# Routing each batch inside the transformer part, with fixed regions of the row buffer for each expert

## The chip, the cores and the metric

The kernel runs on one NeuronCore of a Trainium2 chip. Its time is the device time of one execution in microseconds (us), lower is better. Engines are TensorE (PE; PEld is its weight load), VectorE (DVE), ScalarE (ACT), GpSimd (POOL) and SyncE (SP, which here issues nearly all DMAs).

## The reference

Eight batches of 512 tokens of width 256 go through two layers. The first has two attentions with quantised operands (self, then cross over a context) and a gated feed-forward. The second has a causal self-attention, a cross-attention, and a mixture of eight experts, of which each token uses its two best:

```python
router_weights = jax.nn.softmax(xf @ rw + rb, axis=-1)
topw, topi = jax.lax.top_k(router_weights, K)          # K = 2
topw = jax.nn.softmax(topw, axis=-1)
combine = jnp.zeros((T, E)).at[jnp.arange(T)[:, None], topi].add(topw)
h = gelu(jnp.einsum('td,edf->etf', xf, w1) + b1[:, None, :])
eo = jnp.einsum('etf,efd->etd', h, w2) + b2[:, None, :]
out = jnp.einsum('etd,te->td', eo, combine)
x = layernorm(x + out)
```

T is 4096 tokens, E 8 experts, D 256 and FF 1024.

## The kernel before

There are two parts, one after the other, each a block in which every engine has its own instruction list; the second starts when all engines have ended the first.

**`transformer`** does everything up to the last layer norm ahead of the experts, in batches. `program_steps` names every job as (kind, batch B, stage s, number n) with the jobs it must follow; `program_order` puts the jobs of all engines into one order, `ORDER`, by list scheduling: at each turn it takes, among the jobs that could start earliest, the one with the longest way to the end (`to_end`), with durations from `TAKES` and `LANDS`. Where TensorE would stand idle for `WARM_GAP`, it inserts a filler multiplication (kind `W`, L1286), which keeps the clock up. Each engine then walks `ORDER` and issues its own jobs, in order, with semaphore waits (`after`). Two streams are interleaved: a quantised attention of one batch (S scores, M and nb the row maximum, E the exponential, Q the quantisation on GpSimd at L1000, T and ev the transposed probabilities) and an exact attention of another (A, am, B, E2, AV2). The stages of a batch are 0, 1 (quantised), 2 (feed-forward), 3, 4 (exact), 5 (the norm ahead of the experts; its kinds are rs, xn, gb on GpSimd). Kind `ST` stores the batch to `mid` in DRAM (L914). The batch itself lives in `X`, three buffers. Weights come through the ring `wring` in pieces of 256 KB, `RING` = 8 pieces in flight: piece i is loaded when piece i - 8 has been used for the last time. SP's list also holds `psk`/`pkk`, the store and reload of split queries and keys; beside each of the first 20 stores it writes 528 KB of empty rows into `rows_in` (`fill_some_rows`, L872).

**`experts`** first routes all 4096 tokens at once. `mid` is loaded back into `moe_x` (L1561); TensorE turns it (L1689) and multiplies it with the router weights (L1701); VectorE finds the two best experts of each token (L1822 to L1851), two multiplications with a triangle and with ones give counts, and from them come `owner`, the expert of each of `BLOCKS` = 39 blocks of 256 rows (`OWNERS_READY`), and `slot_of`, the row of each token's two copies (`SLOTS_READY`). Experts' rows are packed: an expert's first row follows from the counts of all batches. GpSimd then scatters the rows, 128 to an indirect DMA, 64 DMAs (L1640). SP, which has meanwhile issued the weights of four blocks, waits for all of them:

```python
sp.wait_ge(s_r, OWNERS_READY)
for slot in range(WSLOTS):
    load_weights(slot, slot)
sp.wait_ge(s_sc, 16 * 2 * NTILES)
for slot in range(2):
    load_block(slot, slot)
```

Then the loop over 39 blocks: TensorE turns a block's rows (L1717), multiplies with `w1` (L1733), ScalarE applies GELU (L1783), TensorE multiplies with `w2` (L1743), VectorE adds the bias (L1894), GpSimd scatters the result to `rows_out` by token (L1650). A tail gathers both results of each token, adds them with their weights and normalises. Empty rows carry a destination out of bounds, so they are not written.

## Time and profile before

| | |
|---|---|
| median of 3 runs | 3555.44 us (3551.76 to 3558.73) |
| the profiled execution | 3552.56 us |
| its span, first to last instruction | 3550.8 us |
| mean granted TensorE clock | 0.926 |
| busy over the span | PE 85%, PEld 48%, DVE 59%, ACT 54%, POOL 46% |
| end of the last tile of batch 7 | 2699.2 us |
| first instruction of the expert part | 2702.56 us |
| first expert multiplication | 2858.62 us |

Shares over the whole span mix the two parts, so stretches are to be read one by one. A granted clock of 1.00 is 2.4 GHz and 0.50 is 1.2 GHz.

### The profile page before, as it was taken

The numbers are of one execution on the slowest core, as the hardware profiler recorded it, in microseconds if no ns is written. First come the engines' busy times: TensorE is split into PE (matmuls) and PEld (weight loads), VectorE is DVE, ScalarE is ACT, GpSimd is POOL, SyncE is SP. The second block draws the span as 40 slices with busy tenths as digits, with TensorE's granted clock in tenths as the row PEclk, the third lists the DMA queues.
The fourth block names the chain that finished last, engine by engine and source line by source line (L and its number), as shares of the span: only waits on it lengthen the run. The fifth ranks groups of instructions, "written<-read, shape, count | busy, mean of one in ns | idle before, by whom it ended". The sixth has DMA issues, their size and how long they took to land. (4 is left out here: it accounts for less than half of the span.)

```text
span 3550.8 us, 54838 instructions
## 1 busy us (share of the span) xinstructions
PE 3008.0 (85%) x18111; PEld 1698.6 (48%) x18111; DVE 2094.1 (59%) x4305; ACT 1905.0 (54%) x3883; POOL 1631.3 (46%) x2840
## 2 busy tenths in 40 slices
PE   6888999898899998899998889988886079999990
PEld 3435444543544454354445435543435067777770
DVE  4877887786789678778967877765450100000006
ACT  4665767576666767666675767654441022232221
POOL 4655554673666368366636736462221511111114
PEclk9999999999999999999999999889986589999995
DMA  3004221531342142132304222242312434555524
GB/s 87 16 25 108 62 68 31 117 82 39 83 83 54 30 96 53 41 68 62 70 24 101 49 48 61 51 77 52 58 29 69 177 128 161 171 176 164 163 94 142
DMA packets 268695, 290.23 MB, mean 82 GB/s; under 512 B 32366, under 2 KB 254190, under 8 KB 268320
## 3 DMA queue, kind: packets, MB, share of 16 engines
q1 hardware_dynamic: 259904, 270.05, 30.5%
q0 software_dynamic: 6816, 17.06, 1.3%
q8 instruction: 134, 2.20, 0.3%
q14 instruction: 113, 0.93, 0.1%
q10 hardware_dynamic: 1728, 0.01, 0.0%
HBM read 225.70 MB, written 62.97 MB: 81 GB/s over the span
## 5 line engine op out<-in xcount | busy, mean ns | idle before, releaser
L1253 ACT ACTIVATE probs<-ps,nbias,sc 128x512 f32<-128x512 f32 x1024 | 790.8, 778 | 276.0 <-DVE nbias L1134 216.9
L1000 POOL TENSOR_SCALAR pq<-probs,rstep 128x512 f16<-128x512 f32 x1024 | 709.6, 693 | 245.4 <-PE ps L1367 161.2
L1151 DVE TENSOR_REDUCE m<-ps 128x1 f32<-128x512 f32 (+3 forms) x1024 | 561.2, 583 | 292.1 <-PE ps L1393 150.3
L1131 DVE TENSOR_REDUCE nmax<-ps 128x2 f32<-128x1024 f32 x512 | 620.9, 1213 | 93.5 <-PE ps L1359 92.8
L1390 PE MATMUL ps<-kst,qst 96*128 96x512 bf16 (+3 forms) x1024 | 328.9, 352 | 92.3 <-issue 50.6
L1893 DVE COPY to<-moe_in 128x1 uint32 x78 | 12.0, 154 | 648.1 <-PE moe_ps L1743 648.1
L1143 DVE TENSOR_SCALAR big<-ps 128x1024 bf16<-128x1024 f16 x512 | 348.2, 680 | 60.7 <-PE ps L1367 59.5
L1367 PE MATMUL ps<-id,pq 128*128 128x128 f16 x4096 | 329.7, 226 | 47.1 <-DVE big L1143 40.0
L1412 PE MATMUL ps<-qst,kst 108*128 108x512 bf16 (+3 forms) x1024 | 305.8, 352 | 66.5 <-ACT big L1272 31.2
L1367 PEld LDWEIGHTS ps<-id,pq 128*128 128x128 f16 x4096 | 261.3, 101 | 193.5 <-issue 129.1
L1272 ACT ACTIVATE big<-ps 128x512 f32<-128x512 f32 (+3 forms) x640 | 275.0, 482 | 145.1 <-PE ps L1415 93.4
L1783 ACT ACTIVATE hT<-moe_ps,e_b 128x256 f32<-128x256 f32 x312 | 147.0, 473 | 360.1 <-PE moe_ps L1733 360.0
L1650 POOL DMA_INDIRECT rows_out<-yb,to x78 | 76.7, 984 | 532.5 <-DVE yb L1894 528.4
L1733 PE MATMUL moe_ps<-moe_bT,e_w 128*128 128x256 f32 x1248 | 287.5, 388 | 8.6 <-ACT hT L1783 7.7
L1743 PE MATMUL moe_ps<-e_w,hT 128*128 128x256 f32 x1248 | 279.4, 382 | 15.4 <-ACT hT L1783 13.1
L1337 PE MATMUL ps<-xT,wring 128*128 128x512 f32 x512 | 272.3, 640 | 0.5 <-ACT xT L1191 0.2
L1743 PEld LDWEIGHTS moe_ps<-e_w,hT 128*128 128x128 f32 x1248 | 233.9, 190 | 54.7 <-issue 23.4
L1733 PEld LDWEIGHTS moe_ps<-moe_bT,e_w 128*128 128x128 f32 x1248 | 219.9, 190 | 70.0 <-ACT hT L1783 32.8
L1390 PEld LDWEIGHTS ps<-kst,qst 96*128 96x128 bf16 x1024 | 98.0, 99 | 316.3 <-DVE m L1151 176.8
L1359 PE MATMUL ps<-kmask,qi 32*128 32x512 bf16 x1024 | 205.4, 401 | 45.5 <-ACT probs L1253 30.6
L1429 PE MATMUL ps<-big,v_f 128*32 128x512 f32 (+3 forms) x2048 | 231.0, 528 | 2.7 <-ACT big L1272 1.6
L1286 PE MATMUL ps<-idb 128*128 128x512 bf16 x737 | 206.6, 392 | 22.0 <-DVE sc L1048 18.1
(202 smaller groups left out, 4610.0 us busy)
## 6 DMA issues: line engine op xcount, KB each, us to landing
e_w<-in_L_xattn_e_w_dram SPq DMA_DIRECT2D x78, 1024.0 KB, 7.8
wring<-in_L_xattn_ff_w_dram SPq DMA_DIRECT2D x96, 256.0 KB, 2.8
parts<-parts_sb SPq DMA_DIRECT2D x64, 384.0 KB, 3.2
kst<-parts SPq DMA_DIRECT2D x192, 128.0 KB, 4.8
qst<-parts SPq DMA_DIRECT2D x192, 128.0 KB, 5.1
moe_in<-rows_in SPq DMA_DIRECT2D x39, 264.0 KB, 2.7
rows_in<-zero SPq DMA_DIRECT2D x19, 528.0 KB, 4.3
xn<-in_ctx_dram SPq DMA_DIRECT2D x16, 512.0 KB, 3.9
```

The source lines that it names most:

```text
L1000: nc.gpsimd.tensor_scalar(pq[:, u % 2, h, :], probs[:, u % 2, h, :], rstep[:, u % 2, h:h + 1], HALF_ROUND, ALU.mult, ALU.add).then_inc(SIG ...
L1131: nc.vector.tensor_reduce(nmax[:, n % 2, :], ps[:, a:a + 2, :], AX.X, ALU.max, negate=True).then_inc(SIG["M"], 1)
L1143: nc.vector.tensor_scalar(probs_t[:, g % 2, 2 * p:2 * p + 2, :, t * P:(t + 1) * P], PT, -HALF_ROUND, WMAX, ALU.add, ALU.min).then_inc(SIG[ ...
L1151: nc.vector.tensor_reduce(m32[:, g % 2, t, h:h + 1], bank(("A", B, s, n))[:, 0:width], AX.X, ALU.max, negate=True).then_inc(SIG["am"], 1)
L1253: nc.scalar.activation(probs[:, u % 2, h, :], ps[:, BANKS[("S", B, s, u)][h], :], ACT.Exp, bias=nbias[:, u % 2, h:h + 1], scale=sc[:, s:s ...
L1272: last = nc.scalar.activation(ex[:, half, h, j, i0:N], ps[:, from_, i0:N], ACT.Exp, scale=SCALE)
L1337: last = nc.tensor.matmul(bank(e), wt[:, k, (f % 2) * P:(f % 2 + 1) * P], xT[:, k, :], start=(k == 0), stop=(k == KT - 1))
L1367: last = nc.tensor.transpose(PT[:, h, j, :], pq[:, n % 2, h, j * P:(j + 1) * P], id16[:, :])
L1390: last = nc.tensor.matmul(bank(e)[:, 0:width], qst[0:PAIR_ROWS, head, t * P:(t + 1) * P], kst[0:PAIR_ROWS, head, 0:width], start=True, sto ...
L1412: last = nc.tensor.matmul(dst[:, i0:N], kst[0:rows_, head, jt * P:(jt + 1) * P], qst[0:rows_, head, i0:N], start=True, stop=not causal(s))
L1733: last = nc.tensor.matmul(ps[:, f % 2, 0:BLOCK], w1[:, ws, k, f * P:(f + 1) * P], bT[:, slot, k, :], start=(k == 0), stop=(k == KT - 1))
L1743: last = nc.tensor.matmul(ps[:, 2 + 2 * slot + s, 0:D], hT[:, f, s * P:(s + 1) * P], w2[:, ws, f, :], start=(f == 0), stop=(f == FT - 1))
```

## The change

The routing leaves the expert part and becomes ten new kinds of job of stage 6 of each batch in the planned order: `rT`, `dr` (turn the batch's rows and drain them), `rL` (logits), `rl`, `rx`, `rm`, `ry`, `ri` (softmax, two best, weights, destinations), `rP` (prefix counts within the batch, by small multiplications), `rp` (the row of each copy, and the running counts `run`), and eight `sc` (indirect DMAs from GpSimd). An expert no longer has packed rows: expert e owns the fixed region of 4096 rows from 4096 e, and `run` says how far it is filled. `rows_in` has 135 blocks in place of 39, and all of it, with a last part of seven blocks, is filled with empty rows beforehand: 64 fills of 528 KB, eight a batch, and one of 1.9 MB after the last batch's store. `sc` of batch B waits for that batch's eight fills. The transformer part now ends when the last scatter has landed. `X` has four buffers, each row eight elements wider for the destinations; the weight ring has six pieces. The expert part computes `owner` from `run`, and `place`, the block in `rows_in` of each of the 39 blocks; it loads weights 0, row blocks 0 and 1, weights 1 to 3, and only then `mid`, which only the tail needs.

```diff
+REGION = TOKENS // BLOCK
+ALL_BLOCKS = NE * REGION + NE - 1
+X_DEEP = 4
...
-RING = 8
+RING = 6
...
-ON = {"PE": "W S T AV A MT B AV2 xT cT k q v y g w z",
-      "DVE": "M nb R ev am n1 n3 st dy dz ki qi vi dV dw",
-      "ACT": "E do mt E2 dT dc dk dq dv dg ge",
-      "POOL": "Q ms n2 rs xn gb bi spk spq",
+ON = {"PE": "rT rL rP W S T AV A MT B AV2 xT cT k q v y g w z",
+      "DVE": "rl rm ri rp M nb R ev am n1 n3 st dy dz ki qi vi dV dw",
+      "ACT": "dr rx ry E do mt E2 dT dc dk dq dv dg ge",
+      "POOL": "sc Q ms n2 rs xn gb bi spk spq",
...
+TAKES = {"rT": 0.49, "dr": 0.66, "rL": 1.4, "rl": 0.55, "rx": 0.25, "rm": 1.2, "ry": 0.25, "ri": 2.2, "rP": 0.6, "rp": 1.0, "sc": 1.25,
...
-        step("LX", B, 0, 0, ("ST", B - 3, 5, 0) if B >= 3 else None)
+        step("LX", B, 0, 0, *((("ST", B - X_DEEP, 5, 0), ("sc", B - X_DEEP, 6, 2 * NT - 1)) if B >= X_DEEP else ()))
...
+        for m in range(KT):
+            step("rT", B, 6, m, ("gb", B, 5, NT - 1), B and ("rL", B - 1, 6, 0))
+            step("dr", B, 6, m, ("rT", B, 6, m))
+        step("rL", B, 6, 0, ("dr", B, 6, KT - 1))
+        step("rl", B, 6, 0, ("rL", B, 6, 0), B and ("rp", B - 1, 6, 0))
+        step("rx", B, 6, 0, ("rl", B, 6, 0))
+        step("rm", B, 6, 0, ("rx", B, 6, 0))
+        step("ry", B, 6, 0, ("rm", B, 6, 0))
+        step("ri", B, 6, 0, ("ry", B, 6, 0))
+        step("rP", B, 6, 0, ("ri", B, 6, 0))
+        step("rp", B, 6, 0, ("rP", B, 6, 0))
+        for n in range(2 * NT):
+            step("sc", B, 6, n, ("rp", B, 6, 0), *(("ps" + which, B, z, m) for which in "kq" for z in (3, 4) for m in range(KT)))
...
+                if B >= X_DEEP:
+                    sp.wait_ge(s_stored, 16 * (B - X_DEEP + 1))
+                    sp.wait_ge(s_sc[B % X_DEEP], 16 * 2 * NT * (B // X_DEEP))
+                sp.dma_start(X[:, B % X_DEEP, :, 0:D], x[B].rearrange("(t p) d -> p t d", p=P)).then_inc(s_x[B % X_DEEP], 16)
...
+            def fill_rows(e, c):
+                first, many = (e * TOKENS + c * N, NT) if c < NBATCH else (NE * TOKENS, (NE - 1) * BLOCK // P)
+                sp.dma_start(every_row[first:first + many * P, :].rearrange("(p n) d -> p n d", p=P),
+                             zero[:, :].unsqueeze(1).broadcast_to([P, many, ROW])).then_inc(s_zeroed[c], 16)
...
-                    fill_some_rows()
+                    fill_rows(filled[0] % NE, filled[0] // NE)
+                    filled[0] += 1
...
+            fill_rows(0, NBATCH)
+            sp.wait_ge(s_zeroed[NBATCH], 16)
+            for i in range(X_DEEP):
+                sp.wait_ge(s_sc[i], 16 * 2 * NT * ((NBATCH - i + X_DEEP - 1) // X_DEEP))
...
+                if kind == "sc":
+                    k, t = n // NT, n % NT
+                    after(pool, "rp", B, s)
+                    pool.wait_ge(s_zeroed[B], 16 * NE)
+                    nc.gpsimd.indirect_dma_start(rows_in.rearrange("b r d -> (b r) d"),
+                                                 bass.IndirectOffsetOnAxis(ap=slot_of[:, B, k, t:t + 1], axis=0),
+                                                 X[:, B % X_DEEP, t, :], None).then_inc(s_sc[B % X_DEEP], 16)
...
+                if kind == "rl":
+                    after(dve, "rL", B, s)
+                    rest_loaded(dve)
+                    then(nc.vector.tensor_tensor(lg[:, :, :], bank(("rL", B, s, 0))[:, 0:NT * NE].rearrange("p (t e) -> p t e", e=NE),
...
+                if kind == "rp":
+                    after(dve, "rP", B, s)
+                    filled = bank(("rP", B, s, 0))
+                    then(nc.vector.tensor_tensor(pos[:, :, :], filled[:, 0:NT * NE].rearrange("p (t e) -> p t e", e=NE),
+                                                 every_tile(run[:, :]), ALU.add), 1)
+                    then(nc.vector.tensor_tensor(run[:, :], filled[:, NT * NE:(NT + 1) * NE], run[:, :], ALU.add), 2)
+                    for k in range(2):
+                        last = nc.vector.tensor_tensor(at_pos[:, k, :, :], eq[:, k, :, :], pos[:, :, :], ALU.mult)
+                    then(last, 3)
+                    then(nc.vector.tensor_reduce(slot_f[:, :, :], at_pos[:, :, :, :], AX.X, ALU.add), 4)
+                    then(nc.vector.tensor_copy(slot_of[:, B, :, :], slot_f[:, :, :]), 5)
...
+                if kind == "dr":
+                    src = ("rT", B, s, n)
+                    after(act, *src)
+                    if n == 0 and B:
+                        after(act, "rL", B - 1, s)
+                    nc.scalar.activation(rT[:, n, :], bank(src), ACT.Identity).then_inc(SIG["dr"], 1)
+                if kind == "rx":
+                    after(act, "rl", B, s)
+                    nc.scalar.activation(pr[:, :, :], lg[:, :, :], ACT.Exp).then_inc(SIG["rx"], 1)
+                if kind == "ry":
+                    after(act, "rm", B, s)
+                    nc.scalar.activation(e1[:, :], dlt[:, :], ACT.Exp).then_inc(SIG["ry"], 1)
...
+                if kind == "rT":
+                    after(pe, "gb", B, 5, NT - 1)
+                    bank_free(pe, e)
+                    for t in range(NT):
+                        last = nc.tensor.transpose(bank(e)[:, t * P:(t + 1) * P], X[:, B % X_DEEP, t, n * P:(n + 1) * P], id32[:, :])
+                    last.then_inc(SIG["rT"], 1)
+                if kind == "rL":
+                    after(pe, "dr", B, s, KT - 1)
+                    rest_loaded(pe)
+                    bank_free(pe, e)
+                    for t in range(NT):
+                        for k in range(KT):
+                            last = nc.tensor.matmul(bank(e)[:, t * NE:(t + 1) * NE], rT[:, k, t * P:(t + 1) * P], rw[:, k, :],
+                                                    start=(k == 0), stop=(k == KT - 1))
+                    last.then_inc(SIG["rL"], 1)
+                if kind == "rP":
+                    after(pe, "ri", B, s)
+                    bank_free(pe, e)
+                    flat = chosen[:, :, :].rearrange("p t e -> p (t e)")
+                    nc.tensor.matmul(bank(e)[:, 0:NT * NE], earlier[:, :], flat, start=True, stop=False)
+                    for t in range(1, NT):
+                        nc.tensor.matmul(bank(e)[:, t * NE:NT * NE], ones[:, :], flat[:, 0:(NT - t) * NE], start=False, stop=(t == NT - 1))
+                    for t in range(NT):
+                        last = nc.tensor.matmul(bank(e)[:, NT * NE:(NT + 1) * NE], ones[:, :], flat[:, t * NE:(t + 1) * NE],
+                                                start=(t == 0), stop=(t == NT - 1))
+                    last.then_inc(SIG["rP"], 1)
...
-            for c in range(NB):
-                sp.dma_start(xs[:, c * NT:(c + 1) * NT, 0:D], mid[c].rearrange("(t p) d -> p t d", p=P)).then_inc(s_x[c], 16)
...
             def load_block(j, slot):
-                sp.dma_start(xin[:, slot, :, :].unsqueeze(1), rows_in[bass.ds(j, 1)].rearrange("a (s p) d -> p a s d", p=P)).then_inc(s_in[slot], 16)
+                b = sp.value_load(place[0:1, bass.ds(j, 1)], min_val=0, max_val=ALL_BLOCKS - 1)
+                sp.dma_start(xin[:, slot, :, :].unsqueeze(1), rows_in[bass.ds(b, 1)].rearrange("a (s p) d -> p a s d", p=P)).then_inc(s_in[slot], 16)
 
             sp.wait_ge(s_r, OWNERS_READY)
-            for slot in range(WSLOTS):
-                load_weights(slot, slot)
-            sp.wait_ge(s_sc, 16 * 2 * NTILES)
+            load_weights(0, 0)
+            sp.wait_ge(s_r, PLACES_READY)
             for slot in range(2):
                 load_block(slot, slot)
+            for slot in range(1, WSLOTS):
+                load_weights(slot, slot)
+            for c in range(NB):
+                sp.dma_start(xs[:, c * NT:(c + 1) * NT, :], mid[c].rearrange("(t p) d -> p t d", p=P)).then_inc(s_x[c], 16)
...
-            pool.wait_ge(s_r, SLOTS_READY)
-            for c in range(NB):
-                pool.wait_ge(s_x[c], 16)
-                for t in range(c * NT, (c + 1) * NT):
-                    for k in range(2):
-                        nc.gpsimd.indirect_dma_start(rows_in.rearrange("b r d -> (b r) d"),
-                                                     bass.IndirectOffsetOnAxis(ap=slot_of[:, k, t:t + 1], axis=0),
-                                                     xs[:, t, :], None).then_inc(s_sc, 16)
...
+            then(nc.vector.tensor_tensor(started_first[:, :, :], started[:, :, :],
+                                         first[:, :].unsqueeze(1).broadcast_to([P, BLOCKS, NE]), ALU.mult))
+            then(nc.vector.tensor_reduce(owner_first[:, :], started_first[:, :, :], AX.X, ALU.max))
+            then(nc.vector.scalar_tensor_tensor(out=place_f[:, :], in0=owner_f[:, :], scalar=float(REGION), in1=iota_b[:, :],
+                                                op0=ALU.mult, op1=ALU.add))
+            then(nc.vector.tensor_tensor(place_f[:, :], place_f[:, :], owner_first[:, :], ALU.subtract))
+            then(nc.vector.tensor_copy(place[:, :], place_f[:, :]))
+            assert steps[0] == PLACES_READY
```

## Rows read from the trace of the kernel before

**Rows 1.** Stretches: us, then busy us of PE, PEld, DVE, ACT, POOL, PE clock, DMA share, GB/s.
```profile
1400.00:1800.00 400.00, 366.39 (x2296) 178.15 (x2292) 313.80 (x601) 266.86 (x516) 220.29 (x400) 0.97 0.28 59
...
2750.00:2800.00 50.00, 1.30 (x6) 0.72 (x5) 18.78 (x136) 0.65 (x2) 21.86 (x23) 0.50 0.62 227
2800.00:2850.00 50.00, 0.00 (x0) 0.00 (x0) 0.00 (x0) 0.00 (x0) 37.86 (x40) 0.50 0.29 106
...
3200.00:3300.00 100.00, 95.41 (x440) 77.91 (x439) 6.71 (x26) 30.84 (x62) 12.79 (x13) 1.00 0.53 172
```

**Rows 2.** The timeline where one part ends and the next begins: start, duration, engine, line.
```profile
2698.49 0.72 POOL L982 TENSOR_TENSOR X<-X,row_l_ln_b 128x256 f32<-128x256 f32 x1
...
2702.56 0.21 POOL L1620 MEMSET moe_id<- 128x128 f32 x1 [3.35 <-POOLq L634]
...
2704.46 0.43 SPq L1559 DMA_DIRECT2D e_b<-in_L_xattn_e_b_dram  x1
...
2712.00 0.10 DVE L1804 MEMSET credit<- 128x1 f32 x2 [22.89 <-DMA e_b<-in_L_xattn_e_b_dram]
```

**Rows 3.** The chain that ended last, from 2700 to 2900: start, duration, what.
```profile
2713.46 3.65 PE moe_ps L1689 x16
2717.11 1.70 PE moe_ps L1701 x16
...
2771.14 85.55 issue
2856.69 1.10 PE moe_ps L1717 x4
...
2858.62 2.08 PE moe_ps L1733 x4
...
2876.78 7.12 PE moe_ps L1733 x32
```

**Rows 4.** The line of the scatter: duration in ns, minimum, median, maximum, then first and last start.
```profile
L1640 POOL DMA_INDIRECT rows_in<-moe_x,slot_of x64: 956/960/1242, 2771.4 to 2851.3; - x64
...
DMA to landing us min/median/max: 2.4/2.4/6.5
```

**Rows 5.** SP's timeline, the stores of batches 0 to 3 to mid.
```profile
689.47 0.37 SPq L914 DMA_DIRECT2D mid<-X  x1
...
1006.38 0.37 SPq L914 DMA_DIRECT2D mid<-X  x1
...
1316.64 0.37 SPq L914 DMA_DIRECT2D mid<-X  x1
...
1630.91 0.37 SPq L914 DMA_DIRECT2D mid<-X  x1
```

**Rows 6.** DMA issues of the page: the zero fills, KB each, median us to landing.
```profile
rows_in<-zero SPq DMA_DIRECT2D x19, 528.0 KB, 4.3
```

**Rows 7.** Timeline of VectorE in the routing: one step on 8, one on 312 elements.
```profile
2765.59 0.17 DVE L1860 TENSOR_SCALAR nblk<-incl 128x8 f32<-128x8 f32 x1
...
2766.41 0.48 DVE L1865 TENSOR_TENSOR started<-iota_b,first 128x312 f32<-128x312 f32 x1
```

**Rows 8.** Owners, first weight load, bandwidth from 2700 to 2900 (5 us each), issues of e_b1.
```profile
2767.66 0.18 DVE L1869 CAST owner<-owner_f 128x39 int32<-128x39 f32 x1
...
2768.86 0.40 SPq L1568 DMA_DIRECT2D e_w<-in_L_xattn_e_w_dram  x1
...
GB/s 107 253 365 357 133 4 0 0 0 3 0 2 0 7 324 385 400 398 409 342 103 106 106 105 102 108 108 108 108 108 86 104 0 0 0 86 332 113 83 329
...
L1563 SPq DMA_DIRECT2D e_b<-in_L_xattn_e_b_dram x8: 582/678/2798, 2716.2 to 2726.0; - x8
```

**Rows 9.** Groups by line, 600 to 2600: count, busy us, mean ns, idle before.
```profile
L1286 PE MATMUL ps<-idb 128*128 128x512 bf16 x376 | 99.6, 386 | 0.9 <-ACT xT L1191 0.9
```

**Rows 10.** Lines of the quantisation (from 600 to 2600) and of nbias: ns minimum, median, maximum.
```profile
L1000 POOL TENSOR_SCALAR pq<-probs,rstep x740: 687/692/715, 600.8 to 2357.0; 128x512 f16<-128x512 f32 x185
...
L1134 DVE TENSOR_SCALAR nbias<-nmax,sc x512: 196/229/1146, 51.7 to 2351.8; 128x2 f32<-128x2 f32 x171
```

299 lines of the change are left out of this document (122 added, 177 removed), and 1 row of the table TAKES.

## The prediction

> **What bounds the kernel now.** I read the stretches first, because an average over the span mixes a transformer part with an expert part. In the transformer part, to 2699 us, TensorE is busy 0.92 of the time (366 of 400 us), VectorE 0.78, GpSimd 0.55; in the expert part TensorE is at 0.95 and sets the pace alone [rows 1]. Between them lie two stretches with TensorE at 0.03 and at nothing, where in the second only GpSimd does anything [rows 1]. That hole is where the change acts. The timeline gives its two ends: the last normalised tile of batch 7 is finished at 2699.21 (2698.49 + 0.72) and stored, and the expert part's first instruction is at 2702.56 [rows 2]. The chain of waits tells what fills the rest: eight batches read back, turned and multiplied with the router weights from 2713.46 on, the choice on VectorE, which ends at 2771.1, and then 85.55 us that the chain can only call issue, until TensorE turns the first block at 2856.69 [rows 3]. The source line of the scatter explains those 85.55 us: 64 indirect DMAs on GpSimd from 2771.4 to 2851.3, one every 1.27 us (79.9 / 63), each landing 2.4 us after its start, and SP loads no block before all have landed [rows 4]. So the path from 2699.2 to the first expert matmul at 2858.62 [rows 3] is serial, and 159.4 us long, of which the expert part's share is 156.1 (from 2702.56).
>
> **What is not on the path.** In the transformer part the period from one batch's store to the next is 316.9 us (689.47 to 1006.38), then 310.3 (to 1316.64) and 314.3 (to 1630.91) [rows 5]. Each batch has eight places for a zero fill and there are 20 fills, so the first of these periods holds eight and the other two none: a fill costs at most (316.9 - 312.3) / 8 = 0.6 us, though 4.3 us pass until it has landed [rows 6]. The change has 44 more of them: at most 25 us, at least nothing; since 310.3 and 314.3 differ by as much without any fill, I take nothing.
>
> **Sum, part 1: the head of the expert part shrinks.** Removed: 8 loads of mid ahead of everything, the 8 turned chunks, the logits, the choice, the 64 scatters. What is left ahead of the first expert matmul, counted from the part's first instruction T0:
> - SP issues the e_b2 load (1 MB) as its third DMA. Before it was the fifth, at 2704.46, and VectorE got past it at 2712.00, 7.5 us later [rows 2]. Two small DMAs earlier (0.95 us), that is T0 + 8.5.
> - VectorE's steps to OWNERS_READY: seven on 8 to 39 elements at 0.17 and two on 312 elements at 0.48 [rows 7], with about 0.04 between: 2.5, so T0 + 11.0. Five more to PLACES_READY, two of them on 312: 1.7, so T0 + 12.7, hidden behind SP.
> - SP reads the owner and issues the first weights 1.0 us after OWNERS_READY, as before (2767.84 to 2768.86) [rows 8]: T0 + 12.0. SP's eight e_b1 issues end before that if they take their median of 0.68 us [rows 8].
> - 2 MB of weights at the 400 GB/s that the queue shows when it is full [rows 8] take 5.2 us, with 2 us of latency 7.2, and the two row blocks (0.5 MB, 1.3 us) are queued behind them: about T0 + 21. I allow 0.5 more for SP's extra register reads.
> - Turning, draining and starting the matmul took 1.9 us (2856.69 to 2858.62): T0 + 23.4.
> So this part gives 156.1 - 23.4 = **132.7 us**. Bounds: the weights 2 us later than 7.2, if the queue is not quite full, and SP late by its e_b1 issues (2716.2 to 2726.0 in this trace, some 10 us for eight behind other loads [rows 8]): 5 us less. Nothing suggests more than 2 us of extra gain.
>
> **Part 2: batch 7's routing now trails the transformer part.** Nothing follows it there that could hide it. From the last tile:
> - 8 transposes, 2 drains, 16 logit matmuls: 0.9 + 0.7 + 1.7 + 0.1 = 3.5 at the fast rate; the rows show 16 transposes in 3.65 at one moment and 16 matmuls in 1.70 at another [rows 3], so a cold TensorE adds up to 2.6.
> - Choice: 24 VectorE instructions on 8 to 32 elements, by the 0.17 of one on 8 [rows 7] about 0.2 with its gap, and one Exp of a like size that is not hidden: 5.0. Eight prefix matmuls at the 0.11 of a logit matmul 0.9; the places, six more small steps, 1.3. Together 10.7.
> - Eight scatters, 7 x 1.27 = 8.9, and 2.4 to land [rows 4].
> That is 22.0 us to T0, with 0.2 for the end of the block, where before it was 3.35: **18.9 us lost**. The last fill (1.9 MB, issued after the store) takes 3.5 x 4.3 = 15 us [rows 6] and ends inside it. Bounds 17 to 24.
>
> **Part 3: routing of batches 0 to 6 inside the transformer part.** Per batch it adds 3.4 us of TensorE, 5.9 of VectorE (25 instructions), 1.7 of ScalarE and 8 x 1.26 = 10.1 of GpSimd, 21 us in all. Its work is nobody's input until the experts, so the planner puts it where an engine would stand idle. Cover: TensorE spends 99.6 us of 2000 on filler multiplications [rows 9], 15.7 a period, besides 0.08 idle; VectorE is idle 0.22 and GpSimd 0.45 of 314 us [rows 1]. Below, the cost is nothing (all in gaps); above, 21 us a batch, if every instruction stood alone on the path. Streams are tightly interlocked: the probabilities quantised on GpSimd (0.69 us each [rows 10]) can have one scatter of 1.27 ahead of each, and eight in a row at worst. I take each instruction to delay its engine's next work by about a fifth of itself, 4 us a batch, nearer to nothing because the eight fills a batch did not show either, and count six batches (batch 6's routing falls after its store, where only batch 7's one stream is left): **24 us lost**. This is the least certain term.
>
> New waits, and what stands behind them: GpSimd's `sc` waits for VectorE's `rp` and for the batch's fills (issued within the batch, long landed), with the quantisation of the next batches behind it, and ScalarE's exponentials behind that; VectorE waits for its own last step 24 times a batch, with row maxima behind; TensorE's `rL` and `rP` wait for ScalarE and VectorE, with every matmul behind. In the plan all are due when reached; the 4 us stand for where they are not. SP's 44 more fill issues stand ahead of the `pkk` reloads, as the first 20 did without a trace in the period. SP's wait of the load of X for scatters is four batches late, so it is free.
>
> **A rule that speaks against part 3.** The 64 scatters that the trace shows ran beside an idle VectorE at 0.96 us [rows 1, 4], and now run beside one busy for 0.78. The nearest row on what the two do to each other: GpSimd's quantisation stays within 687 to 715 ns in 740 cases, while VectorE's tiny nbias takes 196 to 1146 ns [rows 10], so the one that is held up is VectorE, by at most 0.95. If each of 8 scatters did that once, it would be 7.6 us a batch. The Trainium skill (SBUF — State Buffer, on the port pair that VectorE and GpSimd share) says that a DMA issued from GpSimd cannot write its descriptors while VectorE is in a two-port mode, and gives 3100 ns beside one against 620 ns alone. By that page's figures a scatter would take 2.5 us more, 20 us of GpSimd a batch, an estimate; no row here shows it.
>
> **Part 4: small things.** RING 6 in place of 8 loads each weight piece two pieces later; a piece is 256 KB and lands sooner than the 528 KB fill's 4.3 us [rows 6], and a period has 26 pieces, 12 us each, so only the last of a run of pieces is at risk: 0, at worst one wait of 4.3 a batch, 34. Two fewer loads in the start: 0 to 2 us gained, taken as 0. Four X buffers: batch B + 3 is loaded when batch B is stored, a period and more ahead of need, so 0. After the first block, weights 1 to 3 and 4 MB of mid are in the queue ahead of block 2's rows: (6.3 + 4.2) MB / 400 GB/s = 26 us from T0 + 21, so these rows land near T0 + 50, and TensorE wants them 25.3 us after the first matmul (18.2 for block 0, 7.1 into block 1 [rows 3]): T0 + 48.7. **2 us lost**, 0 to 6. From there the expert loop and the tail run as before, with 39 blocks.
>
> **The sum** against the profiled execution's own 3552.6 us (span 3550.8, 2.9 under the median of the runs, 3555.4): 3552.6 - 132.7 + 18.9 + 2 + 24 = 3464.8. I say 3466, for the runs lie a little above the profiled one.
>
> **Rivals.**
> - *All of the routing is hidden* (part 3 nothing): 3552.6 - 132.7 + 18.9 + 2 = 3441. For it: some 40 us of TensorE slack and 140 of GpSimd a period. Against it: a list that is in order and planned with estimates; a mistaken place stalls what is behind it. Chance 0.22.
> - *Routing shows at half its size*, 12 us a batch for six: 3441 + 72 = 3513. Scatters hold VectorE as nbias is held, 7.6, beside the 4 above, or a ring of six makes loads late. Chance 0.15.
> - *Slower than before*: the eight scatters in a row put GpSimd behind, quantisation is late, and with it both streams. The rest of the change gains 3555.4 - 3441 = 114 us, so it takes 114 / 7 = 16.3 us a batch before this decides; GpSimd's added work is 10.1 and all engines' 21, so nearly everything would have to be exposed, or a scatter stretched threefold. At 20 a batch: 3581. Chance 0.05.
> - *The hole is not closed*: something else holds the first block, such as SP's queue. Then perhaps half the 132.7 comes: 3530. Chance 0.03.
> - The forecast, 2 to 8 us a batch: 3464.8, own range 3450 to 3492. Chance 0.55.
>
> **How the numbers follow.** The range takes in the hidden case with the bounds of parts 1 and 2, and reaches to the half-exposed one: 3437 to 3514. Outside it are, above, the slower case, the unclosed hole and half of the half-exposed case (0.05 + 0.03 + 0.08 = 0.16), and below about 0.04 of the hidden one. Within 0.2% of 3555, about what a measurement can tell from no change, there is next to nothing: 0.02, taken from the upper end of the half-exposed case. Slower 0.05, faster the rest, 0.93.
>
> **What would show it.** The hole between the last tile of batch 7 and the first expert matmul should be 22 + 23 = 46 us, not 159. The store of one batch to the next should be 314 + 4 us, and the scatters inside should take about 1 us; if they take 2 or more, the port rule is at work. nbias at a higher mean, or quantisation with longer waits on GpSimd's own earlier work, would show part 3 larger. A wait of TensorE for a weight piece would show RING. The prediction is wrong if the period moves by over 12 us or falls: the planner writes a new order with 20 more jobs a batch, and its quality is not in any row.

## The result: 0.6% faster, not 2.5%

The changed kernel takes 3534.25 us (median of four runs, 3529.76 to 3537.5), the kernel before 3553.6 beside it: a ratio of 0.9942, 95% interval [0.9925, 0.996]. 3466 was predicted, with a range from 3437 to 3514. The profiled execution took 3537.16 us, its span is 3535.2.

The windows of the changed kernel (us, busy us of PE, PEld, DVE, ACT, POOL, PE clock, DMA share, GB/s):

```profile
1400.00:1800.00 400.00, 354.11 (x2294) 183.44 (x2293) 312.85 (x651) 256.74 (x539) 237.08 (x418) 0.92 0.35 78
2784.00:2812.00 28.00, 10.39 (x58) 5.71 (x57) 4.89 (x34) 1.52 (x4) 8.58 (x10) 0.71 0.36 126
2812.00:2836.50 24.50, 1.09 (x4) 0.72 (x4) 3.81 (x18) 0.60 (x1) 0.88 (x7) 0.50 0.76 207
3200.00:3300.00 100.00, 95.40 (x440) 77.91 (x439) 6.71 (x26) 31.31 (x63) 12.80 (x13) 1.00 0.51 163
```

The expert part is what it was. The hole [rows 1] has shrunk to two short stretches. But in the first line TensorE is busy 0.89 of the time instead of 0.92, at a granted clock of 0.92 instead of 0.97, though more is issued to VectorE and GpSimd. So the transformer part runs slower. SP's timeline, the stores to mid of batches 0 to 3 and of batch 7, says by how much:

```profile
692.74 0.37 SPq L963 DMA_DIRECT2D mid<-X  x1
...
1026.32 0.37 SPq L963 DMA_DIRECT2D mid<-X  x1
...
1357.66 0.37 SPq L963 DMA_DIRECT2D mid<-X  x1
...
1689.08 0.37 SPq L963 DMA_DIRECT2D mid<-X  x1
...
2784.85 0.38 SPq L963 DMA_DIRECT2D mid<-X  x1
```

The periods are 333.6, 331.3 and 331.4 us, where [rows 5] gives 316.9, 310.3 and 314.3. The last store stood at 2699.2 before and stands at 2784.85 now: **85.6 us later**, where the sum had 24. The timeline of the hole:

```profile
2784.11 0.72 POOL L1042 TENSOR_TENSOR X<-X,row_l_ln_b 128x256 f32<-128x256 f32 x1
...
2788.70 0.19 DVE L1214 TENSOR_TENSOR lg<-ps,rb 128x32 f32<-128x32 f32 x1 [14.06 <-PE ps L1438]
...
2789.49 0.54 SPq L916 DMA_DIRECT2D rows_in<-zero  x1
...
2796.62 0.17 DVE L1254 CAST slot_of<-slot_f 128x8 uint32<-128x8 f32 x1
2797.09 1.10 POOL L1055 DMA_INDIRECT rows_in<-X,slot_of  x1 [12.26 <-DVE slot_of L1254]
...
2812.61 0.21 POOL L1757 MEMSET moe_id<- 128x128 f32 x1 [5.55 <-POOLq L653]
...
2820.94 0.10 DVE L1886 MEMSET credit<- 128x1 f32 x2 [24.14 <-DMA e_b<-in_L_xattn_e_b_dram]
...
2825.07 0.39 SPq L1701 DMA_DIRECT2D e_w<-in_L_xattn_e_w_dram  x1
...
2836.51 2.07 PE L1826 MATMUL moe_ps<-moe_bT,e_w 128*128 128x256 f32 x4 [0.84 <-ACT moe_bT L1853]
```

From the last tile (2784.83) to the first expert matmul are 51.7 us, not 159.4 [rows 2, 3]. So the account closes: 85.6 lost in the transformer part, 107.7 gained in the hole, 6.5 lost behind it (from the first expert matmul to the end 698.7 us, before 692.2): 15.6 us gained, which is 3550.8 - 3535.2.

One loss behind the hole stands in the chain that ended last:

```profile
2840.34 3.40 SPq L1716
...
2854.81 2.31 SPq L1716
...
2858.33 7.53 DMA moe_in<-rows_in
2865.90 1.12 PE moe_ps L1810 x4
```

SP issues eight loads of mid (L1716) from 2840.34 on, and behind them, at last, block 2's rows, which TensorE turns 29.4 us after its first matmul instead of 25.3.

What doesn't explain the 85.6 us, by source line (ns minimum, median, maximum):

```profile
L1055 POOL DMA_INDIRECT rows_in<-X,slot_of x64: 959/1012/1417, 801.9 to 2806.1; - x64
...
L1067 POOL TENSOR_SCALAR pq<-probs,rstep x738: 688/697/736, 600.6 to 2438.8; 128x512 f16<-128x512 f32 x185
...
L1261 DVE TENSOR_SCALAR nbias<-nmax,sc x367: 195/229/951, 602.4 to 2433.6; 128x2 f32<-128x2 f32 x184
```

and the fills in the page's DMA issues (KB, median us to landing):

```profile
rows_in<-zero SPq DMA_DIRECT2D x64, 528.0 KB, 5.0
```

A scatter takes 1.01 us instead of 0.96, the quantisation 697 ns instead of 692, nbias 229 as before [rows 4, 10]. A fill lands in 5.0 us instead of 4.3 [rows 6]. None of these got slow by an amount that matters.

TensorE is the exception. Here are the windows from batch 2's store to batch 3's, first in the kernel before and then in the changed one, and one line of TensorE in both, from 1000 to 2000:

```profile
1316.64:1630.91 314.27, 284.70 (x1867) 143.89 (x1863) 245.89 (x483) 211.94 (x435) 180.13 (x328) 0.96 0.29 60
1357.66:1689.08 331.42, 293.65 (x1883) 149.35 (x1881) 255.52 (x517) 213.96 (x439) 188.40 (x335) 0.92 0.32 73
...
L1379 PE MATMUL ps<-big,v_int 128*32 128x512 bf16 x400 | 29.7, 383 | 0.9 <-DVE big L1143 0.9
...
L1544 PE MATMUL ps<-big,v_int 128*32 128x512 bf16 x388 | 34.1, 438 | 0.9 <-DVE big L1270 0.9
```

Of the 17.1 us that this period grew, TensorE is busy for 9.0 and idle for 8.1. The same multiplications take longer on the mean (383 to 438 ns in this line), at a granted clock of 0.92 instead of 0.96. So about half of the growth may come with the lower clock, an estimate from these rows; no run below separates it.

### The profile page after: what moved, and what is told of

It reads as the page before. It is cut to its first block and busy times, and to the rows that moved or that the text cites. A ratio compares the mean times of both kernels' runs of the same rounds, so it can differ in the third digit from the quotient of the medians.

```text
span 3535.2 us, 55404 instructions
## 1 busy us (share of the span) xinstructions
PE 3041.9 (86%) x18150; PEld 1705.6 (48%) x18150; DVE 2136.7 (60%) x4455; ACT 1909.7 (54%) x3897; POOL 1638.1 (46%) x2842
## 5 line engine op out<-in xcount | busy, mean ns | idle before, releaser
L1555 PE MATMUL ps<-kst,qst 96*128 96x512 bf16 (+3 forms) x1024 | 337.3, 361 | 108.3 <-issue 63.0
L1413 ACT ACTIVATE big<-ps 128x1024 f32<-128x1024 f32 x192 | 188.6, 1026 | 70.5 <-PE ps L1577 67.5
```

The lines of the kernel that those rows point to most:

```text
L1555: last = nc.tensor.matmul(bank(e)[:, 0:width], qst[0:PAIR_ROWS, head, t * P:(t + 1) * P], kst[0:PAIR_ROWS, head, 0:width], start=True, sto ...
```

## The experiments

Fifteen kernels. The last store to mid is the measure of the transformer part, for it leaves the hole and the experts out. Most were executed once. The kernel before, run beside them, took 3545.8 to 3563.6 us, so a single whole time says little under some 10 us. One transformer part was profiled in two executions: last stores at 2784.85 and 2788.66 (the changed kernel, and the run in which only the loads of mid move). That is one pair only; I take differences under 4 us in the last store to mean nothing, and those near it to be weak. Whole times in the table are medians where there were several executions.

| kernel | last store | whole, us |
|---|---|---|
| before | 2699.2 | 3552.6 |
| before, ring of six | 2694.7 | 3548.2 |
| before, 64 fills | 2717.5 | 3571.1 |
| before, 64 fills, late | 2706.7 | 3560.7 |
| before, in the new order | 2742.3 | 3597.1 |
| before, in the new order, transposes late | 2721.2 | 3578.5 |
| changed | 2784.9 | 3534.3 |
| changed, no scatters | 2767.0 | - |
| changed, fillers twice | 2829.1 | 3594.8 |
| changed, transposes late | 2760.5 | 3511.9 |
| changed, fills late | 2768.4 | 3518.4 |
| changed, mid's loads spread | 2788.7 | 3535.1 |
| changed, all three | 2745.5 | 3493.3 |
| kept order | 2803.0 | 3554.4 |
| kept order, fills late, mid spread | 2786.2 | 3534.4 |
| the same, no scatters | 2754.1 | - |
| the same, routing late | 2740.3 | 3489.0 |

### Parts of the change, put into the kernel before

**Ring of six.** The edit is `RING = 6`.

> The kernel before with a weight ring of six pieces and nothing else. Measured between the changed kernel and the one before: 333.6, 331.3, 331.4, 331.9 us from one batch's store to the next, against 316.9, 310.3, 314.3, 314.1. Theory A (the planned order: the new jobs displace others): no effect here, 310 to 317. Theory B (the routing's own instructions, the scatters above all): no effect either. Theory C (transfers: weights that come late, fills ahead of the reloads): periods of 318 to 325 and waits of TensorE for wring.

The last store came at 2694.7, 4.5 us earlier, about the size of the noise. No cost of the ring shows, as the prediction took it.

**64 fills.** Each of the 64 stores to scratch is followed by a fill.

```
-                if unfilled:
-                    i = unfilled.pop(0)
...
-                    sp.dma_start(to[:, i:i + n, :], zero[:, :].unsqueeze(1).broadcast_to([P, n, ROW])).then_inc(s_zeroed, 16)
+                i = filled[0]
+                filled[0] += 1
+                sp.dma_start(every_row[i * N:(i + 1) * N, :].rearrange("(p n) d -> p n d", p=P),
+                             zero[:, :].unsqueeze(1).broadcast_to([P, NT, ROW])).then_inc(s_zeroed, 16)
```

> The kernel before with 64 fills of 528 KB, eight in every batch, in place of 20, and a row buffer of 135 blocks; everything else as before. Theory C: each fill stands ahead of a reload of split keys or queries, so periods of 320 to 330. Theories A and B: as in the first period of before, which has eight fills, at most 317.

The last store is 18.3 us late (periods of 316.6 to 321.1 us behind the first). "Nothing", in the prediction, was wrong. SP's timeline between the stores of batches 2 and 3, in the kernel with 64 fills, and the matmul that waits:

```profile
1581.24 0.37 SPq L895 DMA_DIRECT2D parts<-parts_sb  x1
1581.65 0.54 SPq L871 DMA_DIRECT2D rows_in<-zero  x1
1582.36 0.53 SPq L895 DMA_DIRECT2D parts<-parts_sb  x1
1582.93 1.29 SPq L871 DMA_DIRECT2D rows_in<-zero  x1
...
1585.61 3.69 SPq L909 DMA_DIRECT2D kst<-parts  x6
...
1589.87 2.78 SPq L909 DMA_DIRECT2D qst<-parts  x6
...
1603.09 0.27 PE L1390 MATMUL ps<-kst,qst 96*128 96x128 bf16 x1 [9.07 <-issue]
```

Two fills, 1 MB, stand in the queue ahead of the reloads kst and qst, and TensorE waits for the stack 9.07 us, in what the profile calls issue. In the kernel before the same place has no fill, and TensorE waits 7.08 us:

```profile
1577.89 2.78 SPq L909 DMA_DIRECT2D kst<-parts  x6
...
1581.25 2.78 SPq L909 DMA_DIRECT2D qst<-parts  x6
...
1593.51 0.27 PE L1390 MATMUL ps<-kst,qst 96*128 96x128 bf16 x1 [7.08 <-issue]
```

From the first reload to the matmul are 15.6 us without the fills and 17.5 with them.

**64 fills, late.** The fill is issued behind the six reloads of its slot instead of ahead of them.

```
                     sp.dma_start(scratch[...]..., parts[:, slot % 2, :, :])
-                    fill_some_rows()
...
                         sp.dma_start(dst[DH * c:DH * (c + 1), 8 * n:8 * n + 8, :], ...)
+                    fill_some_rows()
```

> The kernel before with 64 fills, as in the run of 64 fills, but each issued behind the six loads back from scratch instead of ahead of them. Theory (a fill costs by what stands behind it on the sync engine's queue: the reload of the shifted rows, for which the groups wait): most of the 18.3 us by which the last store was late goes, last store near 2702 (within 4 us of before's 2699.2), whole near 3555 us. Rival (the fills cost by their bytes, 1.9 MB in 64 pieces that share the DMA engines with weights and stacks): last store stays near 2717, whole near 3570 us.

The last store came at 2706.7: 10.8 of the 18.3 us are gone and 7.5 are left, between the theories but nearer to the queue's. The 7.5 may be the bytes; no run shows it. (The bytes are more than the rival says: 44 more fills of 528 KB are 23 MB, and 1.9 MB is the one last fill of the changed kernel.)

**The new order.** The planner of the changed kernel, with its routing jobs, makes the order; those jobs issue nothing there, and routing stays in the expert part.

```
+            step("rT", B, 6, m, ("gb", B, 5, NT - 1), B and ("rL", B - 1, 6, 0))   # and the other routing steps
...
+        if kind in ("rT", "rL", "rP"):
+            continue
```

> The kernel before, with its routing in the expert part, but with the order of jobs that the planner makes for the changed kernel (the new jobs are planned and then issue nothing; X has four buffers as that order needs; the ring stays at eight). Theory A: the order alone makes the period, 325 to 332. Theory B: without the routing's instructions the period is near the old one, 312 to 319, the holes that were left for them being only some us. Theory C: near the old one too.

The periods are 321 to 326 us, between the theories, and the last store is 43.1 us late. The jobs are those of before, in another order on every engine. What differs besides is small: 714 fillers instead of 737, another bank for 56 of the 576 jobs that share the same two banks, and the fourth buffer of `X`. So the plan that was made with the routing in it costs half of the loss with none of the routing's instructions executed.

### Parts taken out of the changed kernel

**No scatters.** The indirect DMA gives way to raising its semaphore.

```
-                    nc.gpsimd.indirect_dma_start(rows_in.rearrange("b r d -> (b r) d"),
...
+                    pool.sem_inc(s_sc[B % X_DEEP], 16)
```

> The changed kernel without its 64 scatters: the rest of the routing stays, rows_in keeps only empty rows, and rows_out is filled with zeros by one DMA at the end of the transformer part, so the result leaves the experts out and the whole time is not to be compared; the periods between stores are. Theory B in the form of scatters that hold GpSimd and VectorE: 318 or less. Theory A: 329 to 332, as if nothing had been taken away. Theory C: 329 to 332.

17.9 us earlier (periods of 328): 2.6 us a batch, for eight scatters of 1.01. The kernel leaves the experts' rows out, so only its transformer part is compared.

**Fillers twice.** Since the granted clock fell from 0.97 to 0.92, one theory was that TensorE pays at the low clock for its stalls. Each filler multiplication is issued twice.

```
                 if kind == "W":
                     bank_free(pe, e)
                     nc.tensor.matmul(ps[:, BANKS[e][0], :], idb[:, :], ..., start=True, stop=True)
+                    nc.tensor.matmul(ps[:, BANKS[e][0], :], idb[:, :], ..., start=True, stop=True)
```

> The changed kernel with each of its 714 filler multiplications issued twice, the order otherwise its own. Time at the low clock ahead of the last store was 263 us before, 392 changed, 355 with the new order alone. Theory D (the new order lets TensorE's clock fall more often, and that is what costs): the low-clock time falls by 50 us or more, and periods from 332 to 326 or less. Theory A' (the order costs by its waits, and the lower clock only follows from them): low-clock time falls, but the periods stay at 331 or grow by the fillers' own time, 90 fillers of 0.22 us a period, to as much as 350.

The first four periods stayed at 331 to 334 us. Ahead of the first store and between the last two, where most fillers stand, they cost: the first store is 22.3 us later and the last two 19.4 us further apart, most of the 44.3 by which the last store is later. The clock over the span rose from 0.925 to 0.932, but from 1000 to 2000, where the periods are, it stayed at 0.92. So theory D was not put to the test: more filler work didn't raise the clock there, and what the lower clock costs stays open.

**Transposes late.** The routing's transposes wait, in the plan, for the next batch's cross-attention projection.

```
-            step("rT", B, 6, m, ("gb", B, 5, NT - 1), B and ("rL", B - 1, 6, 0))
+            step("rT", B, 6, m, ("gb", B, 5, NT - 1), B and ("rL", B - 1, 6, 0), B + 1 < NBATCH and ("y", B + 1, 3, NT - 1))
```

> The changed kernel with one more condition in the plan: a batch's routing starts only after the next batch's self-attention has its output projection (some 30 us later in a period), so its rows are turned and its logits made in one go instead of across 30 us. Theory A (it is where the routing stands in the order that costs, since rT, rL and rP hold one of the two banks that projections and fillers share): 4 us a period or more come back, periods 320 to 328. Theory B (it is the added instructions): 331 as before.

24.3 us earlier (periods of 327 to 329), with all the work of the routing still there. The plan in which it stands matters.

**Fills late**, as above, in the changed kernel; the plan's scatters then depend on the reload too.

```
-            step("sc", B, 6, n, ("rp", B, 6, 0), *(("ps" + which, B, z, m) for ...))
+            step("sc", B, 6, n, ("rp", B, 6, 0), *(("pk" + which, B, z, m) for ...))
```

> The changed kernel with each zero fill issued behind the reload of split keys or queries instead of between the store and the reload. The kernel before lost 18 us by 44 more fills. Theory C (a fill costs because the reload queues behind it): the time ahead of the last store falls by 12 us or more, 2785 to 2773 or less. Rival (the fill costs by its bandwidth wherever it stands): no change within 4 us.

16.5 us earlier, as the theory of the queue says.

**Mid's loads spread** over the last seven blocks.

```
-            for c in range(NB):
-                sp.dma_start(xs[:, c * NT:(c + 1) * NT, :], mid[c]...).then_inc(s_x[c], 16)
+                    if isinstance(j, int):
+                        load_mid()
```

> The changed kernel with the eight loads of mid issued beside the last seven blocks instead of ahead of the block loop. In the changed kernel TensorE waited about 12 us for the rows of block 2 behind them. If that is the queue: the wait is gone and the whole is 10 to 12 us faster, 3523. Rival: SP's own issue time of the weights holds the rows as well, then 4 us or less.

The transformer part is the same code. From the last store to the end are 744.5 us instead of 750.4: 5.8 gained, between the theory (10 to 12) and the rival (4 or less). The wait for block 2's rows is gone; it was 4.7 us, not the 12 that the expectation took it for. The row is of the changed kernel:

```profile
2865.90 1.12 PE L1810 MATMUL moe_ps<-moe_id,moe_in 128*128 128x128 f32 x4 [4.68 <-DMA moe_in<-rows_in]
```

**All three** edits at once, in four executions.

> The changed kernel with the three edits that were tried one by one: the routing's transposes planned behind the next batch's cross-attention projection, the fills issued behind the loads back from scratch, the loads of the middle rows spread over the last seven blocks. Theory (the losses are separate terms: plan 24.3 us, fills 16.5 us, block 2's rows 5.9 us): they add up, last store at 2784.9 - 24.3 - 16.5 = 2744, whole 3534.3 - 22.4 - 15.9 - 5.9 = 3490 us, 1.8% under the kernel before. Rival (late fills and late routing cure the same stall on SP's queue or TensorE's banks, so only the larger counts): last store near 2760, whole near 3506 us.

3493.26 us, ratio 0.9845 [0.9828, 0.9861]; the last store at 2745.5, for 2744 expected. The terms add up, to within the noise.

**The new order, transposes late**: the edit of the late transposes in the plan of the new order, with the kernel before's instructions alone.

> The kernel before in an order of its own instructions that was planned with the routing's jobs in it (which issue nothing), as in the run of the new order, but with the routing's transposes planned behind the next batch's cross-attention projection. Theory (what the new order costs is where the plan puts the routing, whose three kinds of matmul hold one of the two banks that the projections also use): the last store comes some 20 to 25 us earlier than in the new order's 2742.3, near 2720, and the whole near 3575 us. Rival (any plan with the 20 jobs a batch in it is as bad, and the later transposes helped for where the routing's own instructions ran): the last store stays within 8 us of 2742 and the whole near 3597 us.

The last store is at 2721.2: 21.1 of the 43.1 us go by planning the transposes elsewhere, although they aren't executed. What is executed differs only in its order, its banks and some fillers (702), so the place of three kinds of planned job decides how good the order of all the others is.

### The old order, kept

Can the planner's new order of the old jobs be avoided? The plan is made without the routing, which gives the order and banks of the kernel before, job for job; then the routing's jobs are put into places where a bank is free in the plan.

```
+    every = program_steps()
+    steps = {e: behind for e, behind in every.items() if e[2] != 6}
...
-    return order, bank_of
+    return add_routing(every, order, bank_of, begun, ended)
```

> The changed kernel with the main jobs of the transformer part in exactly the order, and in the banks, that they have in the kernel before (the plan is made without the routing); the routing's 20 jobs a batch are put afterwards into places where the plan leaves a bank free, some 36 to 110 us behind the batch's store; 57 of the 737 fillers make room for them. Theory (43 us of the 86 that the transformer part grew by came from the planner's other order of the old jobs): periods fall from 331 to about 322 us, the last store from 2784.9 to about 2742, the whole to about 3493 us. Rival (the routing's matmuls and drains cost the same wherever they stand, since they hold a bank and an engine that the attention needs): the last store stays above 2765 and the whole above 3515 us.

> The same, with the fills issued behind the loads back from scratch and the loads of the middle rows spread over the last seven blocks. Theory (separate terms): last store 2742 - 16.5 = about 2726, whole 3493 - 16 - 6 = about 3471 us, 22 us under the run of all three edits, in which the old jobs stand in another order. Rival (what is left of the loss is the same for both orders): 3485 to 3495 us, as with all three.

The last store is at 2803.0 and, with late fills and spread loads, at 2786.2 (whole 3534.4). In the first run the rival came true (above 2765 and 3515), in the second neither did: the rival had said 3485 to 3495. Against the changed kernel with late fills (2768.4) the kept order is 17.8 us worse. This doesn't clear the planner's order, which costs 43.1 us where hardly anything else changed; it shows that the routing's own instructions, put where this insertion puts them, cost more than the kept order saves. The timeline of the kept order (with late fills), all engines, in batch 4's cross-attention, shows how:

```profile
1411.10 1.48 POOL L1176 TENSOR_SCALAR pq<-probs,rstep 128x512 f16<-128x512 f32 x2 [1.45 <-PE ps L1641]
...
1412.43 0.22 DVE L1370 TENSOR_SCALAR nbias<-nmax,sc 128x2 f32<-128x2 f32 x1
...
1412.68 0.78 ACT L1501 ACTIVATE probs<-ps,nbias,sc 128x512 f32<-128x512 f32 x1 [1.71 <-DVE nbias L1370]
1412.86 1.01 POOL L1164 DMA_INDIRECT rows_in<-X,slot_of  x1 [0.27 <-issue]
...
1416.51 0.77 ACT L1501 ACTIVATE probs<-ps,nbias,sc 128x512 f32<-128x512 f32 x1
...
1417.18 1.01 POOL L1164 DMA_INDIRECT rows_in<-X,slot_of  x1 [0.27 <-POOL pq L1176]
...
1418.28 0.69 POOL L1176 TENSOR_SCALAR pq<-probs,rstep 128x512 f16<-128x512 f32 x1
...
1418.99 0.78 ACT L1501 ACTIVATE probs<-ps,nbias,sc 128x512 f32<-128x512 f32 x1 [0.47 <-POOL pq L1176]
```

Exponential (ScalarE), quantisation (GpSimd), transposes (TensorE), row maxima and nbias, the exponential's bias (VectorE), work in a ring: they hand one head pair to the next and share two buffers of each kind. The exponential of 1416.51 is quantised at 1418.28 only, because the scatter of 1417.18 stands ahead of it, and the exponential of 1418.99 waits 0.47 us for that quantisation. GpSimd is busy 43.9 of 60 us around here, so it has room on the mean; still a part of what it spends otherwise, at the wrong moment, is handed round. All eight scatters of a batch stand between quantisations of this stage; in the changed kernel it is at most one of the eight.

**Routing late, old order kept.** The same kernel, with transposes behind the next projection and the scatters in GpSimd's idle times of the plan, here 126 to 158 us behind the store and behind all quantisations of the cross-attention (in the other 65 to 104 us behind it). 644 fillers are left of 737 (680 in the other), and a filler that stood in the routing's way moves to the other bank where that is free; this edit isn't shown.

```
-            step("rT", B, 6, m, ("gb", B, 5, NT - 1), B and ("rL", B - 1, 6, 0))
+            step("rT", B, 6, m, ("gb", B, 5, NT - 1), B and ("rL", B - 1, 6, 0), B + 1 < NBATCH and ("y", B + 1, 3, NT - 1))
-                pairs = [(e, h if h < ready + 2 else ready)]
+                pairs = [(e, h if e[0] == "sc" or h < ready + 6 else ready)]
```

> The kernel of the kept order with late fills and spread loads of the middle rows, with the routing's jobs at other places: the transposes behind the next batch's cross-attention projection, vector and scalar jobs and above all the scatters only where their engine is idle in the plan (scatters about 110 to 147 us behind the store instead of 53 to 84). The old jobs still stand in the order of the kernel before. New theory (the price is set by where the routing's own jobs stand: in the cross-attention loop, where scores, maximum, exponential and quantisation wait for each other in a ring over four engines, each foreign instruction delays the ring by its whole length; elsewhere it is mostly hidden): the last store comes some 35 to 45 us ahead of the kept order's 2786.2, and the whole near 3495 us, like all three edits together. Rival (the routing's instructions cost their length wherever they stand): last store within 10 us of 2786 and the whole above 3520 us. If the whole is under 3480 us, the planner's own reordering of the old jobs costs something besides.

The last store is at 2740.3, 45.9 us earlier, and the whole at 3488.98, ratio 0.9818 [0.9794, 0.9842]. The windows of both kernels, 50 to 110 us behind the third store (batch 2's) of each, first with the routing in the ring:

```profile
1390.18:1450.18 60.00, 48.94 (x344) 27.86 (x344) 47.50 (x115) 31.54 (x74) 43.92 (x70) 0.87 0.39 89
```

and with the routing late, where no scatter falls into this window:

```profile
1376.56:1436.56 60.00, 52.15 (x384) 31.03 (x374) 52.86 (x124) 37.92 (x89) 40.91 (x73) 0.91 0.45 89
```

In the same 60 us of the batch ScalarE does 89 instructions instead of 74, and TensorE's clock is 0.91 instead of 0.87.

**No scatters, in the kept order.**

> The kernel of the kept order with late fills and spread loads, with no scatter: a semaphore is raised in its place, and the rows that the expert part reads back are filled with zeros at the end, so the result leaves the experts' share out and only the transformer part can be compared. The scatters stand here inside the cross-attention loop, 53 to 84 us behind each store. New theory (a foreign instruction on POOL in that loop costs its full length): eight scatters of 1.04 us plus their gaps of about 0.3 us are 10 us a batch, so the periods fall from 330 to about 320 us and the last store from 2786.2 to about 2720. Rival (they cost what they cost in the changed kernel, 17.9 us in all): last store near 2768.

32.1 us earlier, 4.6 a batch: halfway between what the two theories said. In the ring eight scatters (10.6 us of GpSimd with their gaps) show at nearly half their length; where the planner of the changed kernel puts them they show at a quarter (2.6). "Each by its whole length" was too much.

## Why the prediction was wrong

**What failed is part 3**, the routing of batches 0 to 6 inside the transformer part: 24 us in the sum, 85.6 measured (fills, a term of their own taken as nothing, included). The step that failed is the cover: the prediction let the planner lay the added work into idle places, argued from each engine's idle share and from the filler multiplications, and took each instruction to delay its engine by a fifth of itself; the change of the order of all other jobs it priced at nothing. The runs show in its place:

- The order that the planner makes with the routing in it costs 43.1 us with none of the routing executed.
- The scatters cost 17.9 us where the changed kernel has them, and the fills cost 18.3 in the kernel before, of which moving them gives back 10.8 there and 16.5 in the changed kernel.
- 43.1, 17.9 and 16.5 are 77.5 of the 85.6 us, if they add; that three other edits added up speaks for it, but no run shows it for these.

The loss isn't spread evenly either: the first five periods are longer by 16.7, 21.0, 17.1, 17.8 and 8.8 us, the last two not at all or by 2. A period in which both streams run loses 17 or more where the prediction has 4, and the bound of 21 us a batch for six batches held. Over all, the rival "half its size, 12 us a batch" came nearest: 72 us. The prediction's own sign of being wrong, a period that moves by over 12 us, came true, and it named the planner's order as what is "not in any row"; it gave that too little weight.

The fillers were less cover than the prediction read. It took 15.7 us a period from [rows 9], but that stretch reaches into the last batch's single stream, where they stand close. Within the period between the stores of batches 2 and 3 they are 12.5 us before and 8.4 after:

```profile
L1286 PE MATMUL ps<-idb 128*128 128x512 bf16 x47 | 12.5, 380 | 0.0
...
L1425 PE MATMUL ps<-idb 128*128 128x512 bf16 x32 | 8.4, 381 | 0.1
```

So 4.1 us of fillers went, and the period still grew. One reading, argued and not shown by itself: a filler has nothing behind it that waits, while work of the routing in the same place has a bank, an exponential or a quantisation behind it.

By place, against the kernel before with its 64 fills late, the 21 us a batch of the routing cost 11.4 us a batch when they stood in the ring ((2786.2 - 2706.7) / 7) and 4.8 with the transposes and scatters moved away ((2740.3 - 2706.7) / 7), both with the old jobs in their old order. My 4 us was about right for a good place and not for the one that the planner chose.

Point by point:
- *Part 1, head of the expert part: right.* T0 to the first matmul 23.9 us (2812.61 to 2836.51), 23.4 predicted; VectorE got past e_b2 at T0 + 8.3 (8.5), the first weights went out at T0 + 12.5 (12.0).
- *Part 2, batch 7's tail: mechanism right, 5.6 us too small.* From the last tile to T0 27.8 us instead of 22.2. Transposes to the places took 12.3 (10.7 predicted), the scatters 9.0 (8.9); but from the last scatter's start to T0 it was 6.5 instead of 2.6. It was 6.5 in five other kernels too (transposes late, fills late, mid spread, all three, kept order with the routing late), and the last fill isn't it, with 7.3 us from its issue at 2789.49 to its landing. The mis-sized term is the end of the part, taken as 0.2 us behind a landing of 2.4; what takes the rest isn't shown.
- *Fills: wrong.* Taken as nothing with 25 us as the bound; they cost 18.3 in the kernel before, and their place ahead of the reloads 16.5 in the changed one. The 0.6 us a fill that the periods of before gave as the upper end was nearer (44 x 0.6 = 26) than the lower. The prediction names what stands behind a fill on SP's queue, the reload, and took it as free because the first 20 fills left no trace in the period; it is a stack for which TensorE already waits 7 us.
- *Ring of six: right*, no cost shows. The four X buffers were not tried alone.
- *Block 2's rows: mechanism right*, 2 us predicted, 4.1 of the 6.5 us behind the first matmul, and 5.8 came back when the loads moved.
- *The port rule.* The Trainium skill (SBUF — State Buffer, section "A bandwidth-pool intuition that's wrong") says that a DMA issued from GpSimd takes about 3100 ns beside a `tensor_copy` of VectorE and 620 alone, because it waits for the port. Here the median of 64 scatters, 56 of them beside VectorE at work, is 1012 ns, the longest 1417, against 960 in the idle stretch. The trace doesn't show the rule at work, and it doesn't show either whether VectorE's instructions here take the port; that the prediction left it out of the sum was right.
- *Slower than before: did not come true, but was nearer than thought.* 85.6 us of 114 were eaten.

**What stays open.** That the plan with the routing in it costs 43 us without its instructions is shown, and that half of this goes by planning the transposes elsewhere; which of the old jobs' waits make up the rest isn't. How much of the loss is TensorE's lower clock isn't either: the time at 1.2 GHz ahead of the last store grew from 263 to 392 us, and no run changes the clock of the periods by itself. The kept order with the routing late is still 33.6 us behind the kernel before with 64 late fills, and no run splits that over the engines. The two kernels in the kept order differ in 36 fillers too, besides the places.

The best version found, the kept order with the routing late, late fills and spread loads of mid, is 1.8% faster than the kernel before and 1.3% faster than the changed one (3489.0 against 3534.3).

## What to carry to other kernels

When engines hand work to each other in a ring, the idle share of each is latency and not room: before moving work into it, ask which of the ring's instructions would stand behind it. Here the added work cost about half its length inside the ring and a fourth elsewhere, where the prediction took a fifth everywhere. A large DMA issued "for free" can be paid by the next transfer on its queue that someone waits for: issue it behind that one. And when a planner writes the order, an added job can cost by the order that it brings about for the others: run the new order without the new work, as here, to price it. A constraint of one line in the plan was worth more (24.3 us) than all of the scatters (17.9).

## What had not been expected of the hardware

An indirect DMA issued from GpSimd takes 1.01 us beside a VectorE that is 0.78 busy, 0.05 more than beside an idle one. A zero fill of 528 KB that took 4.3 us to land took 5.0 in the changed kernel and 5.6 in the kernel before with 64 of them; in the place shown, six reload issues of 128 KB behind two of them took SP 3.69 us instead of 2.78. TensorE's granted clock was lower with the stalls (0.97 to 0.92 from 1400 to 1800), yet more filler work (TensorE 897.0 us busy in 1000 instead of 888.4) left it at 0.92 and shortened no period that both streams fill.
